# Flamingo block with gated cross-attention and a routed FFN: the first three FFN up projections moved into attention's last slots

## The chip, the cores and the metric

One NeuronCore of one Trainium2 chip. The metric is the device time of one execution in microseconds; lower is better. Each kernel is timed several times and the median is given.

## What is computed

The input x has 8 batches of 128 tokens and 256 features, the context as much. All arithmetic is f32. First comes grouped-query cross-attention (32 heads of size 8, 8 key groups) with a causal-like mask and a padding mask, then a mixture-of-experts FFN with 16 experts of width 96, of which each token takes two:

```python
q = layernorm(x) @ Wq.T + bq; k = ctx @ Wk.T + bk; v = ctx @ Wv.T + bv
w = softmax(where(mask, -inf, q k / sqrt(8)))
x = x + tanh(g_xattn[0]) * ((w @ v) @ Wo.T + bo)
y = layernorm(x)
probs = softmax(y @ router_w);  weights, idx = top_k(probs, 2);  weights /= sum(weights)
h[e] = silu(y @ gate_w[e]) * (y @ up_w[e])           # for all 16 experts
out = sum_e combine[token, e] * (h[e] @ down_w[e])
x = x + tanh(g_ffn[0]) * out
```

## The kernel before, in words

Every engine has its own instruction stream, written out by hand, and the streams meet only in semaphores. All of them run over the same numbered slots (`SLOTS = 84`). An engine executes its own stream strictly in order, so the place of a step in a stream sets what it waits behind.

Attention has 64 score steps, one per slot from 0 to 63 (8 batches times 8 groups). In a slot TensorE computes the transposed scores of a group (`scores_k`, two matmuls into bank 2 or 3), ScalarE takes their exponential (`pT`, line 688), and TensorE sums values twice a batch (`weigh_values`, bank 4, at slots 5 and 8 of a batch). Up to slot 51 TensorE also computes the plain scores of later batches (`scores_q`, banks 0, 1 and 5), and VectorE takes their maxima (`row_max`, line 869). From slot 52 on banks 0 and 1 are free.

The small jobs stand in a table (`AT_SLOT`) that gives their slot: TO (transposes the attention output of a batch; VectorE divides by the sum), AT (transposes it back; ScalarE and VectorE take a high and a low part), WO (the output projection; VectorE adds it to x and takes the statistics, GpSimd makes the inverse deviation, ScalarE normalises into `xn`), YT (transposes the normalised tile into `xT`, again high and low). Jobs use banks 6 and 7 in turn, and each waits until the job two before it has been emptied. A job issued at slot s is emptied by ScalarE and VectorE at slot s + 1 (`takes_at`).

Routing runs per half (h = 0 or 1, four batches each) by the table `ROUTE`: SC (router scores), SN (transposes them), `best` (VectorE's two largest experts, line 884), `weights` (VectorE's combine weights, line 903), CT (transposes them; VectorE copies them to `comb_t`, SyncE stores this in DRAM and loads it back repeated over partitions as `c_rep`, which lies in the tile `w_t`). The repeated weights have three buffers.

The FFN works on 24 units: 12 tiles of 128 of the 1536 expert rows, times two halves of the tokens, in the order `ORDER`: tiles 0 to 3 of half 0, tiles 0 to 3 of half 1, and then both halves of each tile. A unit is
- `up(n)`, TensorE: gate projection into bank 0 and up projection into bank 1, six matmuls of 512 columns each (three products of high and low parts, two chunks)
- `silu(n)`, ScalarE: bank 0 into `act_g` (line 675)
- `gated(n)`, VectorE: `act_g` times bank 1 into `h_su` (line 929)
- `weigh(n)`, VectorE: times the repeated weights, then a high and a low part (lines 937, 941, 943)
- `down(n)`, TensorE: 12 matmuls of 256 columns, accumulated in banks 2 to 5.

`act_g` and `h_su` lie in attention's tile `pT`, so the first of them can't be written before the last value product (`pv_done` at 16). The tables `UP_SLOT`, `WEIGH_SLOT` and `DOWN_SLOT` give the slots of the first units; `silu(n)` and `gated(n)` follow one slot after `up(n)`. After the last slot the remaining units follow in a loop in which `up(n + 3)` is issued ahead of `down(n)`. GpSimd splits each weight tile in its high and low part (`split_weights`, lines 546 to 551); for tiles from 4 on it waits until the tile four before has been used.

Arithmetic with high and low parts makes three matmuls of each product (`three`, line 1008), all issued from line 1006.

Of the kernel before, what the change touches and what calls it, by code (L numbers as in the profile page):

```python
# [22 lines left out]
NB = 8  # L23
# [10 lines left out]
TH = NT // NQ  # L34
# [13 lines left out]
FT = E * F // P  # L48
UL = 3
WR = 4  # L50
CR = 3
GUC = 2 * DC * P

# [40 lines left out]
def build(nc, x, ctx_in, m_qk, m_pad, g_x, g_f, Wq, bq, Wk, bk, Wv, bv, Wo, bo, Rw, Gw, Uw, Dw, consts, pick, out):  # L94
    es = ExitStack()
    with es:
# [90 lines left out]
        def gu_view(t, flat):  # L187

            return t[:].rearrange(flat)[:, 0:WR * GUC].rearrange("p (s m c f) -> p s m c f", s=WR, m=2, c=DC)

        raw_gu = gu_view(c_sb, "p b d -> p (b d)")
        w_gu = [gu_view(t, "p c n -> p (c n)") for t in cT]
        raw_d = padf[:, 0:WR * D].rearrange("p (s n) -> p s n", s=WR)
# [54 lines left out]
        g_done = sem("g_done")  # L248
        u_done = sem("u_done")
        u_free = sem("u_free")  # L250
        a_ok = sem("a_ok")
        h_ok = sem("h_ok")
        y_done = sem("y_done")
# [19 lines left out]
                else:  # L273
                    NORM_SLOT[b] = G * b + k

        ROUTE = {"SC": (48, 73), "SN": (49, 75), "best": (51, 76), "weights": (53, 77), "CT": (55, 79)}
        for k in ("SC", "SN", "CT"):
            for h in range(NQ):
                AT_SLOT[k, h] = ROUTE[k][h]
# [2 lines left out]

        LASTN = {t: max(n for n, (u, _) in enumerate(ORDER) if u == t) for t in range(FT)}

        UP_SLOT = {0: 64, 1: 66, 2: 70, 3: 74, 4: 77, 5: 80, 6: 81}
        WEIGH_SLOT = {0: 66, 1: 70, 2: 74, 3: 77, 4: 83}
        DOWN_SLOT = {0: 68, 1: 72, 2: 76, 3: 78}
        SLOTS = 84
        LATER = sorted(AT_SLOT, key=lambda j: AT_SLOT[j])
        JOBS = PHASE_A + LATER  # L290
# [286 lines left out]
        def _(sc):  # L577
# [88 lines left out]
            def normalise(k, t):  # L666

                sc.wait_ge(rstd_ok, k + 1)
                nc.scalar.activation(xn[:, t], x_sb[:, t], ACT.Identity, bias=nmr[:, t:t + 1], scale=rstd[:, t:t + 1]).then_inc(xn_ok, 1)

            def silu(n):
                sc.wait_ge(g_done, n + 1)
                if n >= 2:
                    sc.wait_ge(u_free, n - 1)
                nc.scalar.activation(act_g[:, n % 2], bank[0][:], ACT.Silu).then_inc(a_ok, 1)  # L675

            for s in range(SLOTS):
                for j in takes_at(s):
                    if j in hn or j[0] == "MT":
                        high(j)  # L680
                    if j == ("kv", 1):
                        take_values(1)
                if s < CH:
                    b, i = s // G, s % G
                    sc.wait_ge(st_done, s + 1)
                    if b and i % 4 == 0:
                        sc.wait_ge(pv_done, 2 * (b - 1) + i // 4 + 1)
                    nc.scalar.activation(pT[:, i // 4, i % 4, :], bank[2 + s % 2][:], ACT.Exp,  # L688
                                         scale=SCALE).then_inc(p_done, 1)
                if s % G == 1 and G < s < CH + G:  # L690
                    copy_o(s // G - 1)
                if s in (4, 5):
                    for t in (2 * s - 4, 2 * s - 3):
                        normalise(1, t)
                for b in range(NB):
                    if s == NORM_SLOT[b]:
                        if b == 0:
                            sc.wait_ge(d_qc[0], 16 * 3 * 4)
                        normalise(NQ + b, b)
                for n, at in UP_SLOT.items():  # L700
                    if s == at + 1:
                        silu(n)
            for n in range(len(UP_SLOT), len(ORDER)):
                silu(n)
# [3 lines left out]
        def _(ve):  # L708
# [209 lines left out]
                nc.vector.tensor_tensor(comb[:, t4], cb1[:, t4], cb2[:, t4], ALU.add).then_inc(comb_ok, 1)  # L918


            def gated(n):

                ve.wait_ge(a_ok, n + 1)
                ve.wait_ge(u_done, n + 1)
                if n == 0:
                    ve.wait_ge(pv_done, 2 * NB)
                if n >= UL:
                    ve.wait_ge(rep_used, n - UL + 1)
                nc.vector.tensor_tensor(h_su[:, n % UL], act_g[:, n % 2], bank[1][:], ALU.mult).then_inc(u_free, 1)  # L929
# [28 lines left out]
            for s in range(SLOTS):  # L958
# [26 lines left out]
                    if s == ROUTE["weights"][h]:  # L985
                        expert_weights(h)
                for n, at in UP_SLOT.items():
                    if s == at + 1:
                        gated(n)
            for n in range(len(DOWN_SLOT), len(ORDER)):  # L990
                if n + 1 < len(ORDER):
# [12 lines left out]
        def _(pe):  # L1004
# [134 lines left out]
            def up(n):  # L1139
# [3 lines left out]
                pe.wait_ge(*emptied(("YT", (h + 1) * TPH - 1)))  # L1143
                if n == 0:
                    pe.wait_ge(max_ok, CH)
                for m, done, free in ((0, g_done, a_ok), (1, u_done, u_free)):
                    if n:
                        pe.wait_ge(free, n)
                    three(bank[m][:], [lambda c, i=i: w_gu[i][:, s, m, c] for i in range(2)],
                          [lambda c, i=i: xT[i][:, c, half(h)] for i in range(2)], DC).then_inc(done, 1)  # L1150
# [72 lines left out]
```

## Time and profile before

| | us |
|---|---|
| median of 3 runs (252.23 to 252.58) | 252.52 |
| profiled execution | 252.51 |
| its span, first to last instruction | 250.6 |
| TensorE busy | 224.0 (89%) |
| VectorE busy | 174.2 (70%) |
| GpSimd busy | 96.5 (38%) |
| ScalarE busy | 94.0 (37%) |

The busy times are sums over the whole span; engines overlap. Mean granted TensorE clock is 0.976 of full speed (2.4 GHz).

### The profile page before, as it was taken

To read this page: it belongs to the slowest core of one execution; us is meant where nothing else is said; L and a number is where in the kernel's file an instruction comes from. 1 tells how busy PE (TensorE), PEld (TensorE's weight loads), DVE (VectorE), ACT (ScalarE), POOL (GpSimd) and SP (SyncE) were. 2 spreads that over 40 slices of the span, in tenths; PEclk is the share of its full clock that TensorE was granted. 3 is DMA by queue.
4 is the path that set the end of the run, shared out by engine and by line. 5 is a ranking of instruction groups with operands and counts; after the bars stand their busy time and mean duration, and the time that the engine had idled before them with its cause. 6 is when DMAs were issued, how large, how long until landed. Compare 5 with 4: busy or idle time off the path is not lost.

```text
span 250.6 us, 3685 instructions
## 1 busy us (share of the span) xinstructions
PE 224.0 (89%) x1219; PEld 158.9 (63%) x1219; DVE 174.2 (70%) x354; ACT 94.0 (37%) x175; POOL 96.5 (38%) x129
## 2 busy tenths in 40 slices
PE   0876498989999999999598899989999999999993
PEld 0752263565555555556334688778888879898992
DVE  2668768648777878776933566948978687775665
ACT  2465157656566665746445521011101010101000
POOL 6356424400608393920811020401999633520000
PEclk9999689999999999999979999999999999999998
DMA  6371611007760302020042000013455521223104
GB/s 202 80 225 31 157 32 24 0 0 166 172 151 19 68 0 63 0 65 0 0 114 84 30 12 1 3 51 122 104 130 130 176 94 43 67 61 83 43 3 167
DMA packets 26274, 18.62 MB, mean 74 GB/s; under 512 B 15600, under 2 KB 22320, under 8 KB 26256
## 3 DMA queue, kind: packets, MB, share of 16 engines
q1 hardware_dynamic: 25952, 18.17, 27.1%
q10 hardware_dynamic: 304, 0.22, 0.4%
q8 instruction: 10, 0.16, 0.3%
q14 instruction: 8, 0.07, 0.1%
HBM read 14.15 MB, written 1.11 MB: 61 GB/s over the span
## 4 chain that ended last, share of the span: by engine, by line
PE 69%; DVE 13%; POOL 6%; DMA 4%; issue 2%; ACT 1%; SPq 1%; ACTq 0%; DVEq 0%; POOLq 0%
PE bank L1006 60%; DVE mneg L869 2%; PE bank L1046 2%; DMA wkv_n<-in_L_xattn_Wv 2%; POOL cT L547 2%; PE bank L1063 2%; POOL cT L546 2%; POOL w_d L551 2%; PE bank L1067 1%; POOL w_d L550 1%; DMA w_t<-comb_d 1%; DVE cb L915 1%; DVE q L941 1%; DVE pT L937 1%; DVE x_sb L999 1%
## 5 line engine op out<-in xcount | busy, mean ns | idle before, releaser
L1006 PE MATMUL bank<-xT,cT 128*128 128x512 f32 x288 | 70.1, 393 | 0.3 <-DVE pT L929 0.3
L1006 PEld LDWEIGHTS bank<-xT,cT 128*128 128x128 f32 x288 | 52.6, 188 | 11.8 <-issue 0.8
L869 DVE TENSOR_REDUCE mneg<-bank 128x4 f32<-128x512 f32 x64 | 43.1, 685 | 14.5 <-PE bank L1006 13.6
L688 ACT ACTIVATE pT<-bank 128x512 f32<-128x512 f32 x64 | 38.2, 599 | 24.6 <-PE bank L1006 23.5
L675 ACT ACTIVATE pT<-bank 128x512 f32<-128x512 f32 x24 | 14.4, 598 | 77.2 <-PE bank L1006 77.2
L1006 PE MATMUL bank<-q,kz 112*128 112x512 f32 x64 | 38.9, 610 | 0.0
L1006 PE MATMUL bank<-w_d,q 128*128 128x256 f32 x288 | 38.5, 284 | 0.3 <-DVE q L943 0.3
L1006 PEld LDWEIGHTS bank<-w_d,q 128*128 128x128 f32 x288 | 37.0, 190 | 2.6 <-issue 1.2
L929 DVE TENSOR_TENSOR pT<-pT,bank 128x512 f32<-128x512 f32 x24 | 16.4, 684 | 21.7 <-PE bank L1006 20.1
L1006 PE MATMUL bank<-kz,q 96*128 96x512 f32 x64 | 26.7, 426 | 4.8 <-DVE mneg L869 3.2
L1006 PE MATMUL bank<-ident_b,cmask 128*128 128x512 bf16 x64 | 25.4, 397 | 1.2 <-ACT q L609 1.2
L477 POOL TENSOR_TENSOR vare<-mv,cst 128x1 f32<-128x1 f32 (+1 forms) x10 | 2.3, 231 | 60.5 <-DVE mv L723 53.1
L1006 PE MATMUL bank<-cmask,ident_b 128*128 128x512 bf16 x64 | 25.1, 392 | 0.0
L937 DVE TENSOR_TENSOR pT<-pT,w_t 128x512 f32<-128x512 f32 x24 | 19.1, 798 | 4.6 <-DMA w_t<-comb_d 4.3
L508 POOL TENSOR_TENSOR kz<-k,cst 112x512 fp32r<-112x512 f32 x16 | 16.3, 1042 | 11.2 <-DVE k L738 6.5
L943 DVE TENSOR_TENSOR q<-pT,q 128x512 fp32r<-128x512 f32 x24 | 19.7, 822 | 0.8
L1006 PE MATMUL bank<-pT,vz 128*32 128x512 f32 x128 | 17.9, 633 | 0.7 <-ACT pT L688 0.7
L550 POOL TENSOR_TENSOR w_d<-padf,zero 128x256 fp32r<-128x256 f32 x12 | 8.5, 705 | 25.6 <-PE bank L1006 25.6
L1006 PEld LDWEIGHTS bank<-kz,q 96*128 96x128 f32 x64 | 12.4, 194 | 8.2 <-DVE mneg L869 4.5
L547 POOL TENSOR_TENSOR cT<-c_sb,cT 128x512 fp32r<-128x512 f32 x12 | 16.9, 1411 | 0.9
L1006 PEld LDWEIGHTS bank<-cmask,ident_b 128*128 128x128 bf16 x64 | 6.2, 98 | 16.8 <-issue 16.4
L941 DVE CAST q<-pT 128x512 fp32r<-128x512 f32 x24 | 15.5, 647 | 1.8 <-PE bank L1006 0.9
(125 smaller groups left out, 277.3 us busy)
## 6 DMA issues: line engine op xcount, KB each, us to landing
w_t<-comb_d SPq DMA_DIRECT2D x16, 192.0 KB, 2.9
w_t<-comb_d SPq DMA_DIRECT2D x16, 128.0 KB, 2.9
padf<-in_L_ffn_down_w SPq DMA_DIRECT2D x12, 128.0 KB, 2.2
c_sb<-in_ctx SPq DMA_DIRECT2D x2, 512.0 KB, 6.5
q<-cT SPq DMA_DIRECT2D x8, 128.0 KB, 2.8
w_t<-comb_d SPq DMA_DIRECT2D x16, 64.0 KB, 2.7
out<-x_sb SPq DMA_DIRECT2D x4, 256.0 KB, 2.4
q<-xn SPq DMA_DIRECT2D x8, 96.0 KB, 2.2
```

The lines of the kernel that those rows point to most:

```text
L508: ins = pool.tensor_tensor(kz[0:KR, s, g], k4[0:KR, hf, toks(b)].bitcast(F32).unsqueeze(1).to_broadcast([KR, GH, L]), cst[0:KR, C_G + GH * ...
L546: step(pool.tensor_tensor(w_gu[0][:, s], gu, zero[:].unsqueeze(2).unsqueeze(3).to_broadcast([P, 2, DC, P]), ALU.add))
L547: pool.tensor_tensor(w_gu[1][:, s], gu, w_gu[0][:, s].bitcast(F32), ALU.subtract).then_inc(w_ok, 1)
L550: step(pool.tensor_tensor(w_d[0][:, s], raw_d[:, s], zero[:].to_broadcast([P, D]), ALU.add))
L675: nc.scalar.activation(act_g[:, n % 2], bank[0][:], ACT.Silu).then_inc(a_ok, 1)
L688: nc.scalar.activation(pT[:, i // 4, i % 4, :], bank[2 + s % 2][:], ACT.Exp, scale=SCALE).then_inc(p_done, 1)
L869: nc.vector.tensor_reduce(mneg[:, r, 4 * hf:4 * hf + 4], bank[SQ_BANK[n % 3]][:].rearrange("p (g k) -> p g k", g=4), X, ALU.max, negate=Tr ...
L929: nc.vector.tensor_tensor(h_su[:, n % UL], act_g[:, n % 2], bank[1][:], ALU.mult).then_inc(u_free, 1)
L937: nc.vector.tensor_tensor(h_all, h_su[:, n % UL], c_rep[:, n % CR], ALU.mult).then_inc(rep_used, 1)
L941: own(nc.vector.tensor_copy(hh[:, n % 2], h_all))
L943: nc.vector.tensor_tensor(hl[:, n % 2], h_all, hh[:, n % 2].bitcast(F32), ALU.subtract).then_inc(h_ok, 1)
L1006: return nc.tensor.matmul(dst, a, b, start=start, stop=stop, skip_group_check=True)
```

## The change

`up(0)`, `up(1)` and `up(2)` move from slots 64, 66 and 70 to slots 53, 56 and 60, into attention. Their results can't stay in banks 0 and 1, nor go to `act_g`, so ScalarE copies the gate half (`keep_gate`) and VectorE the up half (`keep_up`) one slot later into new views: `g_early` in the tile of the keys `k4`, and `u_early` in `xb_sb` (x with the bias added, batches 0 to 5). `silu` and `gated` of these units read the copies. A new table `ACT_SLOT` gives the slot of `silu(n)` and `gated(n)`. The downs move from slots 68, 72, 76, 78 to 65, 67, 69, 70, the weighings from 66, 70, 74, 77 to 65, 66, 68, 70; `up(3)` moves from 74 to 64, `up(4)` from 77 to 74, `up(5)` from 80 to 77, `up(6)` from 81 to 80. Of the first half's routing `weights` moves from slot 53 to 57 and CT from 55 to 59. The amount of matmul work is the same; three copies on ScalarE and three on VectorE are added.

```diff
@@ -48,6 +48,7 @@
 FT = E * F // P
 UL = 3
 WR = 4
+EARLY_UP = 3
 CR = 3
 GUC = 2 * DC * P
 
@@ -188,6 +189,8 @@
 
             return t[:].rearrange(flat)[:, 0:WR * GUC].rearrange("p (s m c f) -> p s m c f", s=WR, m=2, c=DC)
 
+        g_early = k4[:].bitcast(F32).rearrange("p h n -> p (h n)")[:, 0:EARLY_UP * TH].rearrange("p (s n) -> p s n", s=EARLY_UP)
+        u_early = xb_sb[:, 0:6].rearrange("p b d -> p (b d)").rearrange("p (s n) -> p s n", s=EARLY_UP)
         raw_gu = gu_view(c_sb, "p b d -> p (b d)")
         w_gu = [gu_view(t, "p c n -> p (c n)") for t in cT]
         raw_d = padf[:, 0:WR * D].rearrange("p (s n) -> p s n", s=WR)
@@ -248,6 +251,8 @@
         g_done = sem("g_done")
         u_done = sem("u_done")
         u_free = sem("u_free")
+        g_copied = sem("g_copied")
+        u_copied = sem("u_copied")
         a_ok = sem("a_ok")
         h_ok = sem("h_ok")
         y_done = sem("y_done")
@@ -273,7 +278,7 @@
                 else:
                     NORM_SLOT[b] = G * b + k
 
-        ROUTE = {"SC": (48, 73), "SN": (49, 75), "best": (51, 76), "weights": (53, 77), "CT": (55, 79)}
+        ROUTE = {"SC": (48, 73), "SN": (49, 75), "best": (51, 76), "weights": (57, 77), "CT": (59, 79)}
         for k in ("SC", "SN", "CT"):
             for h in range(NQ):
                 AT_SLOT[k, h] = ROUTE[k][h]
@@ -282,9 +287,10 @@
 
         LASTN = {t: max(n for n, (u, _) in enumerate(ORDER) if u == t) for t in range(FT)}
 
-        UP_SLOT = {0: 64, 1: 66, 2: 70, 3: 74, 4: 77, 5: 80, 6: 81}
-        WEIGH_SLOT = {0: 66, 1: 70, 2: 74, 3: 77, 4: 83}
-        DOWN_SLOT = {0: 68, 1: 72, 2: 76, 3: 78}
+        UP_SLOT = {0: 53, 1: 56, 2: 60, 3: 64, 4: 74, 5: 77, 6: 80}
+        ACT_SLOT = {0: 64, 1: 65, 2: 66, 3: 67, 4: 75, 5: 78, 6: 81}
+        WEIGH_SLOT = {0: 65, 1: 66, 2: 68, 3: 70, 4: 83}
+        DOWN_SLOT = {0: 65, 1: 67, 2: 69, 3: 70}
         SLOTS = 84
         LATER = sorted(AT_SLOT, key=lambda j: AT_SLOT[j])
         JOBS = PHASE_A + LATER
@@ -668,7 +674,22 @@
                 sc.wait_ge(rstd_ok, k + 1)
                 nc.scalar.activation(xn[:, t], x_sb[:, t], ACT.Identity, bias=nmr[:, t:t + 1], scale=rstd[:, t:t + 1]).then_inc(xn_ok, 1)
 
+            def keep_gate(n):
+
+                sc.wait_ge(g_done, n + 1)
+                if n == 0:
+                    sc.wait_ge(kz_ok, 2 * NB)
+                nc.scalar.copy(g_early[:, n], bank[0][:]).then_inc(g_copied, 1)
+
             def silu(n):
+                if n < EARLY_UP:
+                    sc.wait_ge(g_copied, n + 1)
+                    if n == 0:
+                        sc.wait_ge(pv_done, 2 * NB)
+                    if n >= 2:
+                        sc.wait_ge(u_free, n - 1)
+                    nc.scalar.activation(act_g[:, n % 2], g_early[:, n], ACT.Silu).then_inc(a_ok, 1)
+                    return
                 sc.wait_ge(g_done, n + 1)
                 if n >= 2:
                     sc.wait_ge(u_free, n - 1)
@@ -698,7 +719,10 @@
                             sc.wait_ge(d_qc[0], 16 * 3 * 4)
                         normalise(NQ + b, b)
                 for n, at in UP_SLOT.items():
-                    if s == at + 1:
+                    if n < EARLY_UP and s == at + 1:
+                        keep_gate(n)
+                for n, at in ACT_SLOT.items():
+                    if s == at:
                         silu(n)
             for n in range(len(UP_SLOT), len(ORDER)):
                 silu(n)
@@ -918,12 +942,21 @@
                 nc.vector.tensor_tensor(comb[:, t4], cb1[:, t4], cb2[:, t4], ALU.add).then_inc(comb_ok, 1)
 
 
+            def keep_up(n):
+
+                ve.wait_ge(u_done, n + 1)
+                nc.vector.tensor_copy(u_early[:, n], bank[1][:]).then_inc(u_copied, 1)
+
             def gated(n):
 
                 ve.wait_ge(a_ok, n + 1)
+                if n < EARLY_UP:
+                    ve.wait_ge(u_copied, n + 1)
+                    if n == 0:
+                        ve.wait_ge(pv_done, 2 * NB)
+                    nc.vector.tensor_tensor(h_su[:, n % UL], act_g[:, n % 2], u_early[:, n], ALU.mult).then_inc(u_free, 1)
+                    return
                 ve.wait_ge(u_done, n + 1)
-                if n == 0:
-                    ve.wait_ge(pv_done, 2 * NB)
                 if n >= UL:
                     ve.wait_ge(rep_used, n - UL + 1)
                 nc.vector.tensor_tensor(h_su[:, n % UL], act_g[:, n % 2], bank[1][:], ALU.mult).then_inc(u_free, 1)
@@ -985,7 +1018,10 @@
                     if s == ROUTE["weights"][h]:
                         expert_weights(h)
                 for n, at in UP_SLOT.items():
-                    if s == at + 1:
+                    if n < EARLY_UP and s == at + 1:
+                        keep_up(n)
+                for n, at in ACT_SLOT.items():
+                    if s == at:
                         gated(n)
             for n in range(len(DOWN_SLOT), len(ORDER)):
                 if n + 1 < len(ORDER):
@@ -1143,8 +1179,10 @@
                 pe.wait_ge(*emptied(("YT", (h + 1) * TPH - 1)))
                 if n == 0:
                     pe.wait_ge(max_ok, CH)
-                for m, done, free in ((0, g_done, a_ok), (1, u_done, u_free)):
-                    if n:
+                for m, done, free, copied in ((0, g_done, a_ok, g_copied), (1, u_done, u_free, u_copied)):
+                    if 0 < n <= EARLY_UP:
+                        pe.wait_ge(copied, n)
+                    elif n:
                         pe.wait_ge(free, n)
                     three(bank[m][:], [lambda c, i=i: w_gu[i][:, s, m, c] for i in range(2)],
                           [lambda c, i=i: xT[i][:, c, half(h)] for i in range(2)], DC).then_inc(done, 1)
```

## Rows read from the trace of the kernel before

**Rows 1.** Page, part 4: the chain that ended last, by engine.

```profile
PE 69%; DVE 13%; POOL 6%; DMA 4%; issue 2%; ACT 1%; SPq 1%; ACTq 0%; DVEq 0%; POOLq 0%
```

**Rows 2.** Busy time by stage: stretch, length, PE, PEld, DVE, ACT, POOL, clock, DMA share, GB/s.

```profile
121.25:136.03 14.78, 11.68 (x62) 5.75 (x60) 7.71 (x17) 8.17 (x16) 4.49 (x8) 0.88 0.28 84
136.03:163.88 27.85, 25.03 (x142) 20.08 (x143) 18.13 (x51) 6.96 (x12) 6.36 (x11) 1.00 0.03 10
163.88:172.63 8.75, 8.75 (x41) 6.98 (x41) 4.23 (x7) 1.80 (x3) 0.00 (x0) 1.00 0.31 97
172.63:200.80 28.17, 28.13 (x163) 24.53 (x162) 23.32 (x28) 3.59 (x6) 22.76 (x20) 1.00 0.49 130
125.97:129.12 3.15, 3.15 (x13) 0.86 (x12) 0.49 (x1) 0.82 (x2) 1.15 (x4) 0.50 0.53 130
```

**Rows 3.** Timeline of TensorE: start, us, instructions, idle before and its releaser.

```profile
124.97 0.60 PE L1093 MATMUL bank<-cst,comb 128*16 128x128 f32 x4 [1.94 <-DVE comb L918]
...
136.03 1.07 PE L1006 MATMUL bank<-pT,vz 128*32 128x512 f32 x8 [0.69 <-ACT pT L688]
...
155.93 0.42 PE L1089 MATMUL bank<-cst,vT 16*128 16x16 f32 x4
...
163.88 0.60 PE L1093 MATMUL bank<-cst,comb 128*16 128x128 f32 x4 [1.53 <-DVE comb L918]
...
174.12 2.91 PE L1006 MATMUL bank<-xT,cT 128*128 128x512 f32 x12
...
176.88 1.59 PE L1006 MATMUL bank<-w_d,q 128*128 128x256 f32 x12
...
178.31 2.91 PE L1006 MATMUL bank<-xT,cT 128*128 128x512 f32 x12
```

**Rows 4.** Timeline of ScalarE, same columns.

```profile
137.16 0.59 ACT L664 COPY o_sb<-bank 128x512 f32<-128x512 f32 x1 [1.19 <-PE bank L1006]
...
137.77 1.28 ACT L675 ACT_TABLE_LOAD   x1
...
149.30 0.60 ACT L669 ACTIVATE xn<-x_sb,nmr,rstd 128x256 f32<-128x256 f32 x1 [3.80 <-POOL nmr L482]
```

**Rows 5.** Timeline of VectorE, same columns.

```profile
140.13 0.69 DVE L929 TENSOR_TENSOR pT<-pT,bank 128x512 f32<-128x512 f32 x1 [4.06 <-PE bank L1006]
...
140.74 0.35 DVE L809 RECIPROCAL rden<-bank 128x32 f32<-128x32 f32 x1
...
141.47 0.68 DVE L937 TENSOR_TENSOR pT<-pT,w_t 128x512 f32<-128x512 f32 x1
...
143.25 0.42 DVE L735 TENSOR_TENSOR aT<-bank,aT 128x256 fp32r<-128x256 f32 x1
...
145.95 0.48 DVE L818 SCALAR_TENSOR_TENSOR x_sb<-bank,tg,xb_sb 128x256 f32<-128x256 f32 x1
...
147.03 0.69 DVE L937 TENSOR_TENSOR pT<-pT,w_t 128x512 f32<-128x512 f32 x1
...
160.46 0.16 DVE L907 TENSOR_SCALAR den<-e 128x4 f32<-128x4 f32 x1
...
163.65 0.68 DVE L929 TENSOR_TENSOR pT<-pT,bank 128x512 f32<-128x512 f32 x1
...
164.51 0.68 DVE L828 COPY comb_t<-bank 16x512 f32<-16x512 f32 x1 [0.18 <-PE bank L1093]
...
170.65 0.69 DVE L937 TENSOR_TENSOR pT<-pT,w_t 128x512 f32<-128x512 f32 x1
```

**Rows 6.** Timeline of GpSimd, same columns.

```profile
160.87 1.04 POOL L546 TENSOR_TENSOR cT<-c_sb,zero 128x512 fp32r<-128x512 f32 x1 [2.19 <-PE bank L1006]
```

**Rows 7.** Timeline of the DMA queue of SyncE, and landings of line 442 there.

```profile
165.22 0.30 SPq L437 DMA_DIRECT2D comb_d<-comb_t  x1
...
166.78 5.36 SPq L442 DMA_DIRECT2D w_t<-comb_d  x8
...
DMA to landing us min/median/max: 2.4/2.8/3.0
```

## The prediction, before the result was known

> **What bounds the kernel now.** I read the page's chain first: 69% of it is TensorE and 13% VectorE [rows 1], so what TensorE must wait for decides. Then the busy times by stage [rows 2]. The kernel falls into slots; by counting the 64 exponentials the stages are: slot 54 to the last value product of attention (121.25 to 136.03 us), from there to CT of the second half (163.88), from there to the first matmul of down(4) (172.63), and the steady part behind it. TensorE is busy 11.68 of 14.78 us in the first at a mean clock of 0.88, 25.03 of 27.85 in the second, all 8.75 in the third, 28.13 of 28.17 in the fourth. So the fourth stage is TensorE's own; there the order of work is the same before and after the change, and it can only be shifted. The change is worth what it does up to the start of down(4), 172.63 us. Third, TensorE's timeline gives the waits [rows 3]: 1.94 us before CT of the first half (for VectorE's combine weights), 0.69 before the last value product, 1.53 before the second CT. Behind the first of these the granted clock is 0.50 for 3.15 us [rows 2], which is 1.2 GHz, and costs some 1.6 us.
>
> **First stage, slots 54 to 64.** Three ups come in: 12 matmuls each, 2.76 us from the first to what follows (174.12 to 176.88 [rows 3]), so 8.3 us are added. All they need is there (YT(3) and the weight tiles long ago, banks 0 and 1 since slot 51). What goes: the CT wait of 1.94 us, since CT comes after up(0), up(1) and four slots, and VectorE needs only about 3.2 us for the weights [rows 5]; and with up(0) in its place TensorE has no gap there, so the half clock goes too: 1.6 us, with half a microsecond of a wait for copy_o(6) in its shadow, 2.1 together. What comes: ups stop the exponentials, which feed the value products and the transposes. Each keep_gate is a copy like the o_sb copy, 0.59 us [rows 4], behind an Exp on ScalarE. After up(0), exp(55) can't start until its scores exist, so the value product of slot 56 waits some 0.4 us. After up(1) the row is scores, exp(57) 0.6 (ScalarE's 512-column or 256-column instructions take 0.6 each [rows 4]), copy_o(6) 0.6, then TO(6): two score pairs (two of an up's twelve matmuls each, 0.46, so 0.9) cover it in part, 0.9 us remain. keep_gate(1) stands in front of exp(58) and of the normalising of tile 5, for which YT(5) waits: 0.6 us. The wait of 0.69 us before the last value product stays. 8.3 - 1.94 - 2.1 + 0.4 + 0.9 + 0.6 = 6.2; I take +6.1, so that the last value product starts at 142.1. The three keep_up copies (0.69 us or less each, the price of the comb_t copy [rows 5]) fall on a VectorE that has no score maxima left to take, and cost nothing here; without that cover they would cost up to 2 us. In all it is two ups' worth of added length for three ups done.
>
> **Second stage, to CT of the second half.** Before, ups 0 to 4 are spread between the downs; after, only up(3), up(4) and up(5) are left, and down(0) to down(3) stand at slots 65, 67, 69, 70 with little between them. Each down needs its unit's gate product and weighing on VectorE. The prices [rows 5]: gate product 0.61 (140.13 to 140.74), TO 0.73 (to 141.47), weighing 1.78 (141.47 to 143.25), WO with its statistics 1.08 (145.95 to 147.03), each low half of a transpose 0.42, of which 0.35 pass before the next starts, as 0.61 do of the gate product's 0.69. So a unit costs VectorE 2.4 us where its down costs TensorE 1.43 (176.88 to 178.31 [rows 3]); I use 1.45. Counted from the start of the last value product: it ends at 1.05; the table load of 1.28 us [rows 4] runs beside it behind the last Exp; silu(0) 1.25 to 1.85. Then VectorE's queue, in its written order: gated(0) to 2.5, weigh(0) 4.3, gated(1) 4.9, TO(7) 5.6, weigh(1) 7.4, gated(2) 8.0, AT(7) 8.35, gated(3) 8.95, YT(6) 9.3, weigh(2) 11.1, WO(7) 12.2, weigh(3) 14.0. TensorE issues down(0) at 4.3 when up(3) and TO(7) are just over, but then waits about 1.4 us for each of down(1), (2) and (3): down(3) runs 14.05 to 15.5. YT(7) is queued behind it, though its tile was ready (statistics 12.2, plus 2.27 us over GpSimd to the normalising [rows 4, 5]). YT(7) and its two halves 1.4 (0.2 for the transposes, 0.4 a half, the handovers), SC half an up and its handover 1.45, up(4) 2.76: SN at 21.15. From SN to CT took 7.95 us before (155.93 to 163.88 [rows 3]), of which 1.78 was weigh(2), now done: 6.15. CT starts at 27.3, against 27.85. Between SN and CT TensorE has only up(5), 2.8 us, where it had down(2), up(4) and down(3); it idles some 3 us there. So this stage is 0.55 us shorter though two ups fewer (5.5 us) lie in it. Bounds: if TensorE alone set it, 27.85 - 5.5 - its present idle 2.8 = 19.5; if nothing overlapped better than now, 27.85 + 1.
>
> The weights of the second half keep their price of 3.2 us (160.46 to 163.65 [rows 5]): GpSimd splits tile 4 beside them [rows 6], and after the change it again does so, since it waits for the same dif before.
>
> **Third stage, to down(4).** down(4) needs the repeated weights of unit 4: CT, comb_t copy and store issue at +1.34 (165.22), first repeat issued +1.56 (166.78), the second of the unit's two issues about 0.6 later, landing at most 3.0 after it [rows 7], so 6.3 after CT at the latest; weigh(4) to down(4) 1.98 (170.65 to 172.63). Sum 8.3. Before, up(5), up(6) and up(7) filled 8.75 us; now only up(6) and up(7), 6.0. So this stage is 8.3, not 6.0: TensorE idles 2.3 us for the repeat. It shortens by 0.45 only. Bounds: 6.0 if the repeats land early, 9.0.
>
> Sum: +6.1 - 0.55 - 0.45 = +5.1. The chains touch at ideal handovers, but I used rounded-up waits in the first stage, and the repeats may land a little earlier than 3.0; I take +4.9. The profiled execution took 252.51 us (span 250.6, 1.9 around it) and the median is 252.52, so **257.4 us**. Waits added on copied semaphores cost nothing: keep_gate and keep_up are over one slot after the up they follow and the next up comes two to four slots later. The steady part starts as it did: weigh(5) directly behind weigh(4), GpSimd's splits behind down(4), so it is shifted whole.
>
> **Rivals.**
> (a) Table load late. If the load of 1.28 us starts only once silu(0)'s wait for the last value product is met, silu(0) begins at 2.35 and not 1.25, and VectorE's queue, which binds to the end of the stage, moves by 1.1: 258.5. For it: silu(0) now stands in front of copy_o(7). Against: in the kernel before, the load starts at 137.77, right behind copy_o(7), before gate 0 can be complete [rows 4]. The Trainium skill (ScalarE: Activation LUTs, "What ACT_TABLE_LOAD costs") adds a drain of 1.38 us to the load's 1.28; by it silu(0) would start near 2.55 and the time be 258.7. The trace shows no such gap between copy_o(7)'s end and the load. Chance 0.15.
> (b) The clock falls. TensorE's gaps of 3 us before CT and 2.3 before down(4) are longer than the 1.94 behind which the clock was 0.50 for 3.15 us [rows 2, 3]. A fall behind CT hides in the wait for the repeats; a fall at down(4) costs 1.6: 259.0. Against: the 1.53 us gap of the second CT brought no fall (1.00 throughout [rows 2]). The Trainium skill (TensorE: Matmul & The Clock Gate, "What's actually happening") has it that full rate must be earned by activity, and idleness takes it back; that speaks for this case and the trace at 125.97 agrees. Chance 0.15.
> (c) TensorE stays the bound: the reverse sign. If VectorE delivers each unit before TensorE reaches its down, the second stage falls to 19.5 plus 1.5 for CT, the third to 6.0, and the sum is 6.1 - 6.85 - 2.75 = -3.5: 249.0. The point is VectorE's pace per unit in slots 65 to 70: below 1.45 us TensorE leads, above it VectorE does. The rows say 2.4, so only a much looser coupling than I read gives it, for instance gate products and weighings that were slow for another reason. Chance 0.11.
> (d) Half of it: the repeats land early (third stage 6.0) and the second stage gains another 2 us, because handovers I put in series overlap: +1 or, at best, no change, 252.5 to 254.5. Chance 0.12, a third of it within 0.2%.
> The forecast has 0.47.
>
> **How the numbers follow.** 0.2% (0.5 us) is about what can be told from no change. Slower: forecast, (a), (b) and most of (d), 0.84; same 0.04; faster 0.12, from (c) and a little of (d). The range, 254.2 to 259.6, holds the forecast's own spread (third stage 2.3 us less, the fall and the load together 2.7 more less their overlap), and leaves out (c) and the low end of (d).
>
> **What would show it.** Right: the profile shows no wait before the first CT and clock 1.00 from 121 to 130; the last value product near 142.1; waits of over 1 us on TensorE before three of the first four downs, ended by the last step of VectorE's weighing (L943); some 3 us before the second CT, and 2 before down(4), ended by VectorE weighing that waited for the repeat's DMA. Wrong: a second CT before 165 us, downs back to back in slots 65 to 70, or VectorE idle between silu(0) and weigh(3).

## The result and the profile after

| | before | after |
|---|---|---|
| median, us | 252.5 (252.23 to 252.58, 4 runs) | 260.25 (259.6 to 260.84, 4 runs) |
| ratio, 95% interval | | 1.0309 (1.0283 to 1.0334) |
| profiled execution, us | 252.51 | 260.22 |
| its span, us | 250.6 | 258.3 |

The change makes the kernel 3.1% slower. The forecast had the sign and most of the mechanism, but said 257.4 us with a range up to 259.6, and it had the second stage shorter where it came out longer.

The page after, busy times and chain; TensorE's share of the chain fell from 69% [rows 1] to 64%:

```profile
PE 225.5 (87%) x1219; PEld 160.0 (62%) x1219; DVE 174.4 (68%) x357; ACT 95.4 (37%) x178; POOL 95.9 (37%) x129
...
PE 64%; DVE 16%; DMA 6%; issue 4%; POOL 4%; ACT 3%; SPq 1%; ACTq 0%; DVEq 0%; POOLq 0%
```

Busy time by stage (columns as in [rows 2]: length, TensorE, weight load, VectorE, ScalarE, GpSimd, clock, DMA share, GB/s), cut at the same events as there; the first line is the start of the kernel, the second begins at MT(7), half a microsecond before the first cut of [rows 2]:

```profile
24.00:38.00 14.00, 10.61 (x37) 6.23 (x37) 9.59 (x20) 4.29 (x8) 4.60 (x5) 0.63 0.37 85
121.86:143.27 21.41, 19.20 (x101) 12.26 (x101) 7.90 (x22) 9.82 (x19) 5.00 (x9) 1.00 0.20 57
143.27:172.03 28.76, 20.16 (x118) 15.90 (x119) 18.59 (x52) 7.23 (x13) 6.32 (x11) 1.00 0.03 10
172.03:180.36 8.33, 7.68 (x29) 5.94 (x29) 3.63 (x6) 1.20 (x2) 0.00 (x0) 0.80 0.31 103
180.36:208.50 28.14, 28.14 (x162) 24.55 (x162) 24.01 (x28) 3.60 (x6) 22.21 (x20) 1.00 0.47 129
```

Four marks tell the whole difference: the starts of MT(7), of the last value product, of the second CT and of down(4). The stages between them:

| stage | before | after | forecast of the difference | measured |
|---|---|---|---|---|
| start to MT(7) | 120.77 | 121.86 | 0 | +1.1 |
| MT(7) to last value product | 15.26 | 21.41 | +6.1 | +6.15 |
| to the second CT | 27.85 | 28.76 | -0.55 | +0.9 |
| to down(4) | 8.75 | 8.33 | -0.45 | -0.4 |
| to the end | 77.97 | 77.94 | 0 | 0.0 |

TensorE's timeline after, behind the last value product; in brackets stands the idle time in front of the instruction:

```profile
143.27 1.06 PE L1042 MATMUL bank<-pT,vz 128*32 128x512 f32 x8 [0.69 <-ACT pT L709]
144.26 3.06 PE L1042 MATMUL bank<-xT,cT 128*128 128x512 f32 x12
147.16 0.60 PE L1103 MATMUL bank<-cst,o_sb 128*128 128x128 f32 x4
149.11 1.67 PE L1042 MATMUL bank<-w_d,q 128*128 128x256 f32 x12 [1.35 <-issue]
...
152.27 1.66 PE L1042 MATMUL bank<-w_d,q 128*128 128x256 f32 x12 [1.06 <-DVE q L976]
...
155.92 1.67 PE L1042 MATMUL bank<-w_d,q 128*128 128x256 f32 x12 [1.29 <-DVE q L976]
158.80 1.67 PE L1042 MATMUL bank<-w_d,q 128*128 128x256 f32 x12 [1.21 <-DVE q L976]
...
161.73 1.60 PE L1042 MATMUL bank<-xT,rw 128*128 128x512 f32 x6 [1.04 <-DVE xT L759]
...
172.03 0.70 PE L1129 MATMUL bank<-cst,comb 128*16 128x128 f32 x4 [2.65 <-DVE comb L942]
172.39 7.32 PE L1042 MATMUL bank<-xT,cT 128*128 128x512 f32 x24
180.36 1.67 PE L1042 MATMUL bank<-w_d,q 128*128 128x256 f32 x12 [0.65 <-issue]
```

Each of the four downs waits more than 1 us, the last three for the low part of the weighed product; then the router scores wait, then CT. In front of down(0) the profile names no releaser ("issue"), but VectorE's low part of unit 0 ends at 149.01 and down(0) starts at 149.11. VectorE's lines of that unit, the gate product and the first and last step of the weighing:

```profile
146.40 0.69 DVE L957 TENSOR_TENSOR pT<-pT,xb_sb 128x512 f32<-128x512 f32 x1 [3.09 <-ACT pT L691]
147.13 0.69 DVE L970 TENSOR_TENSOR pT<-pT,w_t 128x512 f32<-128x512 f32 x1
...
148.32 0.69 DVE L976 TENSOR_TENSOR q<-pT,q 128x512 fp32r<-128x512 f32 x1
```

The 1.94 us wait in front of the first CT [rows 3] is gone. The two ups behind the second CT take 7.3 us and not 5.7: the clock fell behind the wait of 2.65 us (0.80 in that stage), which eats most of the wait for the repeated weights, so only 0.65 us of idle time is left there. after_2 and after_3, two more profiles of the changed kernel, show the same in that stage (7.68 and 7.70 us busy at a clock of 0.79 and 0.80).

### The profile page after: what moved, and what is told of

The parts are those of the page before. It is cut to its first block, busy times and chain, and to the rows that moved or that the text cites. A ratio compares the mean times of both kernels' runs of the same rounds, so it can differ in the third digit from the quotient of the medians.

```text
span 258.3 us, 3693 instructions
## 1 busy us (share of the span) xinstructions
PE 225.5 (87%) x1219; PEld 160.0 (62%) x1219; DVE 174.4 (68%) x357; ACT 95.4 (37%) x178; POOL 95.9 (37%) x129
## 4 chain that ended last, share of the span: by engine, by line
PE 64%; DVE 16%; DMA 6%; issue 4%; POOL 4%; ACT 3%; SPq 1%; ACTq 0%; DVEq 0%; POOLq 0%
PE bank L1042 57%; DMA w_t<-comb_d 3%; DVE pT L970 2%; DMA wkv_n<-in_L_xattn_Wv 2%; DVE mneg L893 2%; PE bank L1099 2%; DVE q L974 2%; PE bank L1082 1%; POOL cT L553 1%; POOL w_d L557 1%; PE bank L1103 1%; POOL w_d L556 1%; POOL cT L552 1%; DVE x_sb L1035 1%; DVE q L976 1%
## 5 line engine op out<-in xcount | busy, mean ns | idle before, releaser
L1042 PE MATMUL bank<-xT,cT 128*128 128x512 f32 x288 | 72.3, 400 | 0.3 <-DVE pT L962 0.3
L1042 PEld LDWEIGHTS bank<-xT,cT 128*128 128x128 f32 x288 | 53.7, 192 | 13.1 <-issue 1.7
L709 ACT ACTIVATE pT<-bank 128x512 f32<-128x512 f32 x64 | 38.1, 599 | 29.0 <-PE bank L1042 28.0
L696 ACT ACTIVATE pT<-bank 128x512 f32<-128x512 f32 x21 | 12.6, 599 | 74.3 <-PE bank L1042 74.3
L1042 PE MATMUL bank<-q,kz 112*128 112x512 f32 x64 | 38.2, 600 | 0.0
L962 DVE TENSOR_TENSOR pT<-pT,bank 128x512 f32<-128x512 f32 x21 | 14.3, 683 | 16.0 <-PE bank L1042 16.0
L970 DVE TENSOR_TENSOR pT<-pT,w_t 128x512 f32<-128x512 f32 x24 | 20.8, 869 | 4.5 <-DMA w_t<-comb_d 4.2
L1042 PE MATMUL bank<-pT,vz 128*32 128x512 f32 x128 | 17.0, 605 | 0.9 <-ACT pT L709 0.9
L974 DVE CAST q<-pT 128x512 fp32r<-128x512 f32 x24 | 14.6, 606 | 1.8 <-PE bank L1042 1.1
```

Source lines behind the costliest of these rows:

```text
L970: nc.vector.tensor_tensor(h_all, h_su[:, n % UL], c_rep[:, n % CR], ALU.mult).then_inc(rep_used, 1)
L974: own(nc.vector.tensor_copy(hh[:, n % 2], h_all))
L1042: return nc.tensor.matmul(dst, a, b, start=start, stop=stop, skip_group_check=True)
```

## The experiments

Times are medians; ratios are to the kernel before on the same chip. Stages are as in the table above.

| kernel | us | ratio (95%) | MT(7) at | to value product | to CT | to down(4) |
|---|---|---|---|---|---|---|
| route_only | 250.9 | 0.994 (0.992 to 0.995) | 120.46 | 12.69 | 27.85 | 8.75 |
| ups_only | 259.4 | 1.026 (1.024 to 1.028) | 121.65 | 20.75 | 28.77 | 8.06 |
| table_early | 258.3 | 1.022 (1.020 to 1.024) | 121.02 | 21.41 | 27.67 | 8.08 |
| spread | 261.3 | 1.035 (1.033 to 1.037) | 121.96 | 21.39 | 28.39 | 9.59, with down(3) |
| light_weigh | 258.4 | 1.022 (1.018 to 1.026) | 121.79 | 21.41 | 26.05 | 7.99 |
| rep_early | 258.4 | 1.025 (1.018 to 1.032) | 120.74 | 21.41 | 28.77 | 6.04 |
| route_split | 248.9 | 0.986 (0.983 to 0.990) | 120.83 | 12.70 | 26.16 | 8.75 |
| one_early | 256.3 | 1.015 (1.011 to 1.018) | 121.73 | 15.81 | 30.07 | 8.75 |
| one_early_table | 254.3 | 1.007 (1.005 to 1.008) | 121.27 | 15.80 | 27.64 | 8.75 |
| after_both | 257.7 | 1.020 (1.018 to 1.022) | 120.97 | 21.39 | 25.93 | 8.15 |
| tuned_a | 249.5 | 0.987 (0.986 to 0.989) | 120.75 | 13.71 | 26.17 | 8.76 |
| tuned_b | 248.8 | 0.984 (0.982 to 0.986) | 120.79 | 13.69 | 24.16 | 10.62, with down(3) |

**The two parts alone.** route_only is the kernel before with `"weights": (57, 77), "CT": (59, 79)`; ups_only is the changed kernel with these back at 53 and 55.

> The kernel before with one part of the change alone: the first half's combine weights at slot 57 and CT at 59, no early ups. My account (each of TensorE's waits has its own price): the 1.94 us wait before the first CT and the half clock behind it (1.6 us) go, some of it comes back as the next wait on ScalarE's exponentials; 249.0 to 250.0. Rival 1 (the routing's delay is what costs, through the repeated weights of the first half): 252.5 or more.

> The changed kernel with the first half's routing back at slots 53 and 55. My account: up(0) at slot 53 covers VectorE's combine weights, so the routing's place hardly matters here: 259.5 to 261.0, with less than 0.5 us of wait before the first CT. Rival 1 (the routing's delay is a large part of the loss): under 257.

The routing alone gains: its stage is 2.6 us shorter in the profiles and nothing behind it moves. About half of the 2.6 is the fall of the clock, which one profile of the kernel before doesn't have (before_3 below, 13.98 us: 1.3 longer than 12.69); the medians differ by 1.8 us. The median of 250.9 is 0.9 above the range I gave. The ups alone carry the whole loss; with them in place the routing's move is worth nothing and even costs 0.7 us (21.41 against 20.75), since up(0) already covers VectorE's weights: ups_only has no wait in front of the first CT. The two parts of the change take away the same wait. (259.4 is 0.1 under the range I gave.) Measured against route_only and not against before, the three early ups cost 21.41 - 12.69 = 8.7 us up to the last value product and 0.9 - 0.4 = 0.5 behind it. Nothing is given back. The ups themselves are nearly all of the 8.7: each takes 2.85 us in the profile after, from its start to the next instruction's (122.26 to 125.11, 128.59 to 131.45, 136.39 to 139.23), 8.55 in all. That leaves little for the six copies; no run tests them by themselves.

**The table load.**

```diff
                     nc.scalar.activation(pT[:, i // 4, i % 4, :], bank[2 + s % 2][:], ACT.Exp,
                                          scale=SCALE).then_inc(p_done, 1)
+                    if s == CH - 1:
+                        nc.scalar.activation(tab_w[:], zero[:], ACT.Silu)
```

> The changed kernel with a one-column Silu into a scratch column directly behind the last Exp, so that the table load runs before the last value product is done. My account: silu(0) starts 1.1 us earlier, VectorE's queue up to the second CT moves by the same, 259.1 against 260.2. Rival 2 (VectorE's queue does not set the second stage, the waits of TensorE there come from elsewhere): 260.2, no change.

As expected, the second stage is 1.09 us shorter. The median is 1.9 us below the changed kernel's, 0.8 more than that; the profiled execution starts MT(7) 0.84 us earlier (121.02), which is taken up under the start of the kernel. ScalarE after, around silu(0): the last Exp, the wait for the value product, the load, silu(0):

```profile
142.62 0.60 ACT L709 ACTIVATE pT<-bank 128x512 f32<-128x512 f32 x1 [0.58 <-PE bank L1042]
144.44 1.28 ACT L691 ACT_TABLE_LOAD   x1 [1.23 <-PE bank L1042]
145.74 0.63 ACT L691 ACTIVATE pT<-k 128x512 f32<-128x512 f32 x1
```

The load stood behind silu(0)'s wait, not in front of it as before [rows 4]. The Trainium skill (ScalarE: Activation LUTs, "What ACT_TABLE_LOAD costs") counts 1.38 us of drain besides the load at each switch to another set. The traces show the load's 1.28 us and no such drain: here the load ends at 145.72 and silu(0) starts at 145.74; in the kernel before, where the load comes right behind a copy, it ends at 139.05 and silu(0) starts at 139.06. The measurement decides, and 258.7 by the page's figure in rival (a) falls away.

**Is it VectorE's queue?** light_weigh leaves out one step of VectorE in units 0 to 3:

```diff
+                if n < 4:
+                    nc.vector.tensor_copy(hh[:, n % 2], h_all).then_inc(h_ok, 1)
+                    return
                 own(nc.vector.tensor_copy(hh[:, n % 2], h_all))
...
-                                [lambda c, i=i: (hh, hl)[i][:, n % 2, toks(u)] for i in range(2)],
+                                [lambda c, i=i: (hh, hl if n >= 4 else hh)[i][:, n % 2, toks(u)] for i in range(2)],
```

> The changed kernel with VectorE's last step of weighing (the low part, 0.61 us) left out for units 0 to 3; down() of these units uses the high part in its place, so TensorE's work is the same and the output is not the reference's. My account: VectorE's serial queue sets TensorE's second stage, so each unit gives back 0.6 us there: second stage 28.8 to 26.4, the time 257.8 against 260.2. Rival 2 (TensorE's waits there come from latencies of TensorE, DMA or GpSimd): 260, no change.

The stage shrank by 2.7 us, where I had said 2.4, with TensorE's work unchanged, so VectorE's queue does set it. The four downs still wait, but 0.32 to 0.62 us each and no longer 1.06 to 1.35. The time gave only 1.8, because in this execution the clock fell later, behind down(4), where nothing hides it:

```profile
169.25:177.24 7.99, 6.08 (x28) 4.72 (x29) 3.62 (x6) 1.20 (x2) 0.00 (x0) 1.00 0.32 107
177.24:182.00 4.76, 4.76 (x20) 4.14 (x21) 4.59 (x7) 0.20 (x1) 2.64 (x3) 0.64 0.16 47
```

**An order that I thought better.** spread changes only three tables: `ACT_SLOT` {0: 64, 1: 66, 2: 67, 3: 70, ...}, `WEIGH_SLOT` {0: 65, 1: 69, 2: 71, 3: 78, ...}, `DOWN_SLOT` {0: 66, 1: 70, 2: 72, 3: 80}.

> The changed kernel with only the order behind slot 64 changed: downs at 66, 70, 72, 80 and weighings at 65, 69, 71, 78, so that the last batch's TO, AT and WO stand in front of the weighings on VectorE, and down(3) and weigh(3) come behind the second CT. My account (VectorE's serial queue delays the chain over YT(7), SC and the weights to CT): CT of the second half about 5 us sooner after the last value product (23 to 25 us instead of 28.8), the time 254 to 256. Rival 3 (the six copies and the ups inside attention carry the loss): 259.5 to 260.5, as the copies are all still there.

A miss by 5 us. What failed is seen in TensorE's lines, and it lies in my order; the run can't tell what the copies cost, which rival 3 blamed:

```profile
149.96 0.41 PE L1108 MATMUL bank<-cst,an 128*128 128x128 f32 x2 [2.17 <-DVE an L835]
...
155.98 2.90 PE L1042 MATMUL bank<-w_d,q 128*128 128x256 f32 x12 [3.25 <-DVE q L976]
158.68 0.61 PE L1116 MATMUL bank<-cst,xn 128*128 128x128 f32 x2
159.97 1.67 PE L1042 MATMUL bank<-w_d,q 128*128 128x256 f32 x12 [0.68 <-DVE q L976]
```

The statistics of the last batch were ready 2.8 us sooner (154.0 against 156.8), but down(1) stood in front of YT(7) on TensorE and waited 3.25 us for a weighing that I had put last, and down(2) stood in front of SC in the same way. Behind the second CT, weigh(3) stood in front of the comb_t copy (173.90 against 172.77), so the repeated weights came 1.1 us later. A step freed on one engine gained nothing while its successor was queued behind a starved one on another. How much a better order could give with three early ups stays open.

**The wait for the repeated weights.** SyncE loads unit 4's weights from the first half before it waits for the second CT:

```diff
+                if n == 4:
+                    sp.wait_ge(rep_used, n - CR + 1)
+                    for e, f0, f1, at in pieces(t):
+                        sp.dma_start(c_rep[at:at + f1 - f0, n % CR],
+                                     comb_d[e:e + 1, half(0)].to_broadcast([f1 - f0, TH])).then_inc(d_rep[n % CR], 16)
                 if t == 0:
                     sp.wait_ge(*emptied(("CT", h)))
```

> The changed kernel with the repeated weights of unit 4 taken from the first half, so that weigh(4) doesn't wait for the second CT and its store (the output of this unit is wrong). My account from the profile after: from the second CT to down(4) two limits lie side by side, the repeat (8.3 us) and the two ups at half clock behind the wait of 2.65 us (7.7). So only 0.6 us go: 259.6. If the repeat alone set it: 6.0 us, 257.9.

In the profiled execution the clock did not fall behind CT (two ups in 5.73 us) and the stage is 6.04 us: with both limits gone it is two ups long. light_weigh gives the other half: its clock did not fall behind CT either (1.00), it does have to wait for the repeat, and its stage is 7.99 us. So at full clock the repeat alone holds the stage for 1.95 us. VectorE's first step of weigh(4) in light_weigh waits for it:

```profile
175.26 0.69 DVE L970 TENSOR_TENSOR pT<-pT,w_t 128x512 f32<-128x512 f32 x1 [1.87 <-DMA w_t<-comb_d]
```

The four timed executions of rep_early were 256.95, 257.04, 259.72 and 259.80, two kinds and within 1 us of the two values expected; the profiled one is 256.95, whose MT(7) also starts early (120.74). That the slower two had the fall behind CT would fit their times, but there is no profile of them. Why executions differ is taken up under the start of the kernel.

**Fewer early ups.** one_early is the changed kernel with `EARLY_UP = 1` and all other slots as before; one_early_table adds the early table load.

> Routing as in the changed kernel, but only up(0) early (slot 53), all other ups, downs and weighings at the slots of the kernel before. My account: an early up costs its whole 2.8 us before the last value product, and gives back only what silu(0) and the transposes of the last batch start earlier behind it, 1.5 us: 252.3 against 250.9 of route_only. Rival 4 (the first early up is free because it fills the wait of the first CT; the loss is in the second and third one): 249.5 or less.

> one_early with the one-column Silu behind the last Exp. In one_early the table load stood in front of copy_o(7), with no up on TensorE to cover it, and the clock fell behind the wait. My account: the second stage falls from 30.1 to 26.0 to 26.5, so the early up costs 3.1 us and gives back 1.5: 252.5 (250.9 of route_only + 1.5). Rival 4 (an early up fills a wait and is free): 249.5 or less.

Both missed: 256.3 against 252.3 expected, and 254.3 against 252.5. The price of the one up up to the last value product is 15.81 - 12.69 = 3.1 us, where the first text said 2.8. The larger miss is in what it gives back. In one_early the table load stood in front of copy_o(7), and TensorE had no up to issue meanwhile; it waited 2.65 and 1.00 us and the clock fell:

```profile
141.26 1.09 PE L1103 MATMUL bank<-cst,o_sb 128*128 128x128 f32 x4 [2.65 <-ACT o_sb L670]
143.35 0.66 PE L1108 MATMUL bank<-cst,an 128*128 128x128 f32 x2 [1.00 <-DVE an L835]
143.66 4.94 PE L1042 MATMUL bank<-xT,cT 128*128 128x512 f32 x12
```

The three-up kernel has up(3) there, which covers it. With the load early the second stage is 27.64, so the up gives back 0.2 us, not 1.5: TensorE still waits 1.53 for copy_o(7) and 1.00 for the division, again at lowered clock (the up behind takes 4.15 us). Even one early up is a loss of some 3 us by the stages (3.1 - 0.2), 3.4 by the medians, so rival 4 is out.

**GpSimd beside VectorE.** route_split is route_only with one more wait; after_both is the changed kernel with this and the table load.

```diff
                 if t >= WR:
+                    if t == WR:
+                        pool.wait_ge(comb_ok, 2)
                     pool.wait_ge(u_done, LASTN[t - WR] + 1)
```

> route_only, and GpSimd's split of weight tile 4 waits until the second half's combine weights are done on VectorE. My account: VectorE's combine weights take 3.2 us beside GpSimd's split and 1.4 us without (first half in the profile after); the 1.5 us wait before the second CT goes, and 1.5 us of the time: 249.4 against 250.9. Rival: the price of these VectorE steps does not hang on GpSimd, or the split comes too late for up(8): 250.9 or more.

> The changed kernel with both small mends: the early table load and GpSimd's split of tile 4 behind the second combine weights. My account adds the two in the second stage: 28.8 - 1.1 - 1.8 = 25.9, and the wait before the second CT shrinks to 0.9; 257.3. Still 8 us above route_split, since the ups' 8.7 us in attention are paid and VectorE's queue sets what follows. If it came under 254, my account of the ups would be wrong.

route_split is 1.7 us shorter up to CT and the wait in front of it is gone; 248.9 against 249.4 expected. Two of VectorE's steps in route_only, and GpSimd's split beside them:

```profile
157.99 1.07 DVE L911 TENSOR_SCALAR w<-inv,tg 128x4 f32<-128x4 f32 x1
...
159.22 1.38 DVE L915 TENSOR_TENSOR cb<-cb,w 128x64 f32<-128x64 f32 x2
```

```profile
157.99 1.04 POOL L546 TENSOR_TENSOR cT<-c_sb,zero 128x512 fp32r<-128x512 f32 x1 [2.19 <-PE bank L1006]
159.11 1.27 POOL L547 TENSOR_TENSOR cT<-c_sb,cT 128x512 fp32r<-128x512 f32 x1
```

The same two steps in route_split, with the split behind them:

```profile
158.37 0.23 DVE L913 TENSOR_SCALAR w<-inv,tg 128x4 f32<-128x4 f32 x1
...
158.76 0.36 DVE L917 TENSOR_TENSOR cb<-cb,w 128x64 f32<-128x64 f32 x2
```

The slowed steps end with GpSimd's instruction or soon behind it: the first at 159.06 beside 159.03, the pair at 160.60 beside 160.38. The Trainium skill (GPSIMD Engine Reference, "Specifications") says that GpSimd shares its SBUF interfaces with VectorE and contends with VectorE's instructions in a 2-port mode or with two SBUF inputs. The pair has two SBUF inputs, and it agrees (0.36 alone, 1.38 beside GpSimd); the first step reads one tensor and a column of factors and is slowed as well (0.23 to 1.07), and no run shows in which mode it ran.

In after_both the two mends add as expected (25.93, and 0.96 us of wait in front of the second CT), and the time is 257.7 against 257.3 expected: mending the surroundings leaves the ups' cost.

**Further moves on route_split.** tuned_a: `"best": (52, 76)` and (11, 13, 15, 18, 19) for batch 6. tuned_b: besides, `up(1)` at 65, `weigh(3)` at 81, `down(3)` at 82.

> route_split and three small moves: the first half's two largest (best) one slot later, behind YT(4)'s emptying; TO and AT of batch 6 one slot later; WO of batch 6 at slot 63, in the wait before the last value product. My account: the waits of 0.94, 0.79 and 0.69 us in front of MT(7), TO(6) and the last value product go for the most part: 246.5 to 247.5 against 248.9. Rival: the same exponentials and copies are only waited for elsewhere: 248.9.

> tuned_a, and up(1) in front of AT(7), where TensorE waits 1.2 us for VectorE; weigh(3) and down(3) behind the second CT, so that the later chain of the last batch finds 1.8 us less in front of its weights. My account: 1.2 us less than tuned_a, 245.5 to 246.5. Rival: the last batch's chain sets the second CT, and the 1.4 us by which up(1) delays it come back as a wait there: as tuned_a or slower.

tuned_a missed (249.5 against 246.5 to 247.5), its rival held and more: the 0.94 in front of MT(7) went, but TensorE waits 1.03 for the normalised tile 5 and 0.49 for its low half instead, as the later slots put ScalarE's and VectorE's part of the chain behind; from MT(7) on it is 1.0 us longer than route_split. tuned_b missed too (248.8 against 245.5 to 246.5): it gained 0.4 us of span on tuned_a, 0.7 by the medians, and not 1.2. Its second CT comes 2.0 us sooner, but down(3) now lies behind it. route_split and tuned_b, 0.986 and 0.984, can't be told apart; both beat both kernels, by 3.5 to 3.9 us against before.

**The start of the kernel.** Both kernels once more, unchanged.

> The kernel before, unchanged, profiled again. If the first stretch of half clock belongs to the program, the mean clock from 24 to 38 us is 0.76 again and MT(7) starts near 120.8; if to the execution, 0.63 and MT(7) near 121.8 turn up, and then the time of 252.5 must have won the 1.1 us back elsewhere, most likely at the wait before the first CT.

> The changed kernel, unchanged, profiled again. Program: clock 0.63 from 24 to 38 us and MT(7) at 121.9. Execution: also 0.76 and 120.8 can turn up, with a time near 259.2.

> As before_2. A third profile of the kernel before: with three of one kind against seven of nine kernels with early ups of the other kind, chance alone would be unlikely; a mixture shows chance.

> As after_2. The place of MT(7) tells the kind; the stage from there to the last value product should be 21.4 us in every one of them, and from there on 28.8, 8.0 to 8.4 and 77.9.

| execution | us | clock 24 to 38 | MT(7) | to value product | clock falls at 126 |
|---|---|---|---|---|---|
| before | 252.51 | 0.76 | 120.77 | 15.26 | yes |
| before_2 | 252.66 | 0.63 | 121.04 | 15.10 | yes |
| before_3 | 252.25 | 0.63 | 121.81 | 13.98 | no |
| after | 260.22 | 0.63 | 121.86 | 21.41 | no |
| after_2 | 260.07 | 0.63 | 121.79 | 21.37 | no |
| after_3 | 259.94 | 0.63 | 121.45 | 21.41 | no |

It belongs to the execution, not to the program: the same kernel before has both clocks at its start. The lines of before_3 for the start and for slots 53 to 64, to be compared with 0.88 in [rows 2]:

```profile
24.00:38.00 14.00, 10.62 (x37) 6.17 (x37) 9.59 (x20) 4.36 (x8) 4.60 (x5) 0.63 0.37 85
121.81:135.79 13.98, 10.57 (x64) 5.93 (x64) 8.17 (x19) 8.18 (x16) 4.97 (x9) 1.00 0.33 89
```

Of the nine kernels with early ups eight show 0.63 or 0.64 there in their first profile. The two values are not two clean kinds: before_2 has 0.63, yet its MT(7) starts at 121.04, only 0.27 us behind before and 0.77 ahead of before_3, and its half clock lies earlier (a mean of 0.51 from 24 to 28 us, where before_3 has 0.68).

before_3 starts its MT(7) 1.04 us later than before and has no fall behind the first CT wait, which is 1.28 us shorter to the last value product; its time is that of the others. Of three executions of before, none had both the short stretch at the start and no fall at 126, so 252.5 was the time in each. The changed kernel has no wait there, so it can't win that back; what it could have is the short start, and in three profiles it had it in none. Other kernels did: the profiles of route_only, rep_early and route_split have 0.76, and each is the fastest execution of its kernel. Why the clock falls in one execution and not in another, whether the two stretches have to do with each other, and how often the short start comes, stays open.

## Why the prediction was off

Right, with the numbers of the table: the first stage as a sum (+6.15 for +6.1), the third (-0.4 for -0.45), the steady part (0.0). The first of these is in part luck: each up took 2.85 us and not 2.76, and the three waits behind the ups came to 0.23, 0.78 and 0.40, 1.41 us in all where I took 1.9. The third stage's limit by the repeat is real (7.99 us in light_weigh, 6.04 in rep_early), but in the changed kernel the two ups at lowered clock took up most of it. Right in kind: VectorE's queue as the limit behind slot 64 (light_weigh), with waits of 1.06 to 1.29 us on three downs where 1.4 was said, 2.65 in front of CT where 3 was said. The rival of opposite sign, (c), needed a unit of VectorE under 1.45 us; the downs start 2.9 to 3.7 us apart.

The step that failed is in the second stage: "the table load of 1.28 us runs beside it behind the last Exp; silu(0) 1.25 to 1.85". silu(0) started at 2.47 after the start of the value product. That was rival (a), with 2.35 and a price of 1.1; table_early measured 1.09. With 0.35 us more, below, it made the stage 0.9 us longer instead of 0.55 shorter. I gave the rival 0.15 because the load before ran ahead of a wait. There silu(0) waited for one semaphore, and in the changed code it waits for two; that this is why the load moved was not tested apart. The other 0.35 us of the stage also lie in front of down(3), which starts 15.53 after the value product and not 14.05: 0.12 in silu(0) (2.47 for the rival's 2.35), 0.12 where weigh(0) waits for its own gate product (0.73 us, 146.40 to 147.13, where I took 0.61), and the rest in the last weighing and its handover. From down(3) to CT it took 13.23, as forecast (13.25).

The second step is the starting point: my sum stood on one execution, and took off 1.6 us for a fall of the clock that this execution had and before_3 has not (with the wait for copy_o(6) that it hides, the fall cost 1.3 us: 15.26 - 13.98). Against before_3 the first stage costs +7.4; against the profiled one it costs +6.15 and 1.1 us come up front. Up to the last value product both give nearly the same total, 7.2 and 7.5, and the sum without the clock's term comes nearer to before_3's +7.4 than 6.1 does: 8.3 - 1.94 + 0.4 + 0.9 - 0.5 (the wait for copy_o(6)) + 0.6 = 7.8. Rival (b) came true in the hidden form that the text gives it; a fall at down(4), its costly form, is in light_weigh's and after_both's executions. Last, I shaved 0.2 us off the sum without a row. 4.9 + 1.1 (table) + 0.35 + 1.1 (clock) + 0.2 is 7.65 of the 7.7 measured.

The range failed because what came together, (a), the clock at the start and two small terms, all stood on the same side and made 2.75 us, and I let it end 2.2 above the forecast.

## What to carry to other kernels

Before moving TensorE work to an earlier stretch, ask whether TensorE is idle there and whether the stretch that it leaves is TensorE's own. In this kernel neither held. The later stretch was held by a chain over VectorE, GpSimd and a DMA; the moved ups had been its cover, and taking them out turned cover into waits. To clear a wait, first try to move the awaited step alone (route_only), and look what runs on another engine beside the steps that are late (route_split). Where one profile shows a fall of the clock, take a second profile before its price goes into a sum.

## What the runs showed of the hardware

- The clock's falls differ between executions of one program: before fell at 126 us in two of three profiles, and the half-clock stretch at the start, between 24 and 38 us, had a mean of 0.76 in four profiles and of 0.63 or 0.64 in all others, with the same instructions. MT(7) started between 120.46 and 120.83 us with the first, between 120.97 and 121.96 with the second (tuned_a and tuned_b, which lack the wait in front of it, left out).
- A wait of 2.65 to 2.69 us on TensorE before the second CT was followed by a lowered clock behind CT in six profiles (the three of the changed kernel, ups_only and table_early, 0.79 to 0.80 in the stage; spread, where the up behind it takes 4.59 us), and by full clock there in rep_early and light_weigh.
- Small VectorE instructions beside a GpSimd operation and without one: a product of 4 columns 1.07 us (route_only) and 0.23 (route_split), an addition of 4 columns 1.00 (after, 168.77) and 0.17 (route_split), two products of 64 columns 1.38 and 0.36.
- The place of a table load differs with the code around it: directly behind a copy and before gate 0 was complete where silu(0) waited for one semaphore (137.77 in the kernel before), and 0.1 us behind the value product's end where it waited for two (144.44 in the changed kernel; the same in ups_only and one_early). That the number of waits is the reason is my reading of the code.
